# A decoder layer on one core: value products one step later, and qk, v and the rotary k in other steps

## The reference, cut to what matters

```python
x = _layernorm(x + _L0_attn_ref(x, w_project, w_out))        # causal, 16 heads of 16
x = _layernorm(x + _L0_xattn_ref(x, ctx_2048, Wq, bq, Wk, bk, Wv, bv, Wo, bo))
x = _layernorm(x + _L0_ffn_ref(x, w1, b1, ln_g, ln_b, w2, b2))
...
# cross attention: x and ctx are (32, 64, 256), read as 64 channels of length 256
q = _apply_rotary(q_emb, split_heads(_proj(x, Wq, bq)))      # 8 heads of 8 channels
k = _apply_rotary(k_emb, split_heads(_proj(c, Wk, bk)))
v = split_heads(_proj(c, Wv, bv))
p_attn = softmax(einsum('bhtc,bhsc->bhts', q, k) / sqrt(8))  # 256 x 256 per head
out = _proj(einsum('bhts,bhsc->bhtc', p_attn, v))
```

## Time and profile before

| what | value |
|---|---|
| profiled execution | 563.8 us, span 561.9 us |
| PE busy | 450.6 us (80%) |
| DVE busy | 442.4 us (79%) |
| ACT busy | 382.0 us (68%) |
| POOL busy | 289.6 us (52%) |
| mean granted TensorE clock | 0.848 |

### The profile page before, as it was taken

How to read it: one execution, slowest core, us unless ns; L and a number is a source line. 1 busy time by engine, 2 the same in 40 slices (tenths; PEclk the granted TensorE clock), 3 DMA queues, 4 the chain that set the end, 5 groups by cost and what they waited for, 6 DMA issues and landing times. The chain is left out here.

```text
span 561.9 us, 12026 instructions
## 1 busy us (share of the span) xinstructions
PE 450.6 (80%) x4162; PEld 243.0 (43%) x4162; DVE 442.4 (79%) x965; ACT 382.0 (68%) x698; POOL 289.6 (52%) x387
## 2 busy tenths in 40 slices
PE   6568799999999999999999999889877701555563
PEld 5354545555545555555555555433333200333342
DVE  2656687888988979889889798865848959999973
ACT  2222266767767667676676686687767787999972
POOL 5742565447555574475555744620032727667652
PEclk9677799999999999999999999975987875555555
DMA  6134318233242242332422323210000000000010
GB/s 217 48 97 149 97 46 248 66 92 91 57 111 67 64 110 60 90 91 60 108 69 64 106 61 82 71 56 1 3 1 1 1 0 1 10 28 19 30 37 29
DMA packets 51674, 37.07 MB, mean 66 GB/s; under 512 B 21408, under 2 KB 47648, under 8 KB 51488
## 3 DMA queue, kind: packets, MB, share of 16 engines
q1 hardware_dynamic: 51328, 36.10, 22.8%
q10 hardware_dynamic: 288, 0.23, 0.2%
HBM read 24.52 MB, written 10.49 MB: 62 GB/s over the span
## 5 line engine op out<-in xcount | busy, mean ns | idle before, releaser
L970 DVE TENSOR_REDUCE MX<-mx_b 128x2 f32<-128x512 f32 x256 | 167.8, 679 | 37.6 <-PE mx_b L581 36.4
L775 ACT ACTIVATE PB<-e_b 128x512 f32<-128x512 f32 x256 | 149.6, 592 | 64.7 <-PE e_b L609 63.8
L581 PE MATMUL mx_b<-KA,QA 48*128 48x256 bf16 x512 | 100.8, 282 | 10.3 <-DVE MX L970 10.1
L609 PE MATMUL e_b<-QA,KA 50*128 50x256 bf16 x512 | 100.9, 281 | 2.7 <-ACT PB L775 2.1
L626 PE MATMUL u_b<-PB,VA 128*32 128x256 f32 x1024 | 86.2, 404 | 3.4 <-ACT PB L775 2.9
L897 POOL TENSOR_TENSOR SP<-SP,srec 128x1024 f32<-128x1024 f32 x15 | 28.5, 1901 | 79.0 <-DVE srec L942 79.0
L581 PEld LDWEIGHTS mx_b<-KA,QA 48*128 48x128 bf16 x512 | 30.1, 95 | 88.5 <-issue 48.9
L1238 POOL TENSOR_TENSOR H<-H,row_tab 128x1024 f32<-128x1024 f32 x16 | 37.8, 2359 | 22.9 <-ACT H L1196 19.5
L1285 PE MATMUL r_b<-identh,Q 128*128 128x128 f16 x128 | 16.6, 311 | 39.5 <-ACT Q L1206 39.5
L1291 PE MATMUL z_b<-w2q,Q2T 128*128 128x256 bf16 x128 | 30.2, 417 | 19.3 <-ACT Q2T L1217 19.3
L314 POOL TENSOR_TENSOR rs<-mv,epsc 128x1 f32<-128x1 f32 x32 | 6.1, 189 | 72.5 <-DVE mv L301 50.2
(11 more groups left out here) (169 smaller groups left out, 1048.4 us busy)
## 6 DMA issues: line engine op xcount, KB each, us to landing
KA<-parts_k SPq DMA_DIRECT2D x64, 96.0 KB
QA<-parts_q SPq DMA_DIRECT2D x64, 96.0 KB
parts_q<-part_q SPq DMA_DIRECT2D x32, 128.0 KB, 2.0
parts_k<-part_k SPq DMA_DIRECT2D x16, 192.0 KB, 2.1
C<-in_ctx SPq DMA_DIRECT2D x16, 128.0 KB, 3.0
X<-in_x SPq DMA_DIRECT2D x16, 128.0 KB, 2.9
out_y<-O SPq DMA_DIRECT2D x16, 128.0 KB, 1.7
XT<-in_xT SPq DMA_DIRECT2D x15, 128.0 KB, 2.2
```

The source lines that it names most:

```text
L581: m = nc.tensor.matmul(mx_b[n % 2][:, D * k:D * k + D], QA[low:low + K_MAX, 2 * i.ring + b, h, P * u:P * u + P], KA[low:low + K_MAX, 2 * i ...
L609: m = nc.tensor.matmul(e_b[n % 2][:, D * k:D * k + D], KA[low:low + K_EXP, 2 * i.ring + b, h, P * sc:P * sc + P], QA[low:low + K_EXP, 2 * ...
L775: nc.scalar.activation(PB[:, n % 4].rearrange("p e t -> p (e t)"), e_b[n % 2][:, :], ACT.Exp, scale=XC ** -0.5).then_inc(e_sb.sem, 1)
L970: nc.vector.tensor_reduce(MX[:, b, e, 2 * q:2 * q + 2, u], mx_b[n % 2][:, :].rearrange("p (e s) -> p e s", e=2), AXL.X, ALU.max).then_inc( ...
```

## The change

On PE the quads 0 to 6 move from the even steps 2 to 14 to the odd steps 3 to 15, each behind the other blocks of its step, and quad 7 of the pair before moves from step 0 to step 1. `qk_proj` moves from step 1 to step 0, `rotary_proj("k")` from step 9 to step 8, `v_proj` from step 12, where it stood ahead of `transpose_p`, to step 14. On ACT the two `u_copy` move from steps 0 and 8 to steps 1 and 9. DVE's, POOL's and SP's lists in a body stay as they are. In the prologue a small table (`identb`) is made by two copies in place of one addition, and the counts of the semaphore s_tab are raised by one.

```diff
-                    if s == 0 and real(prev):
+                    if s == 0 and fresh(a):
+                        qk_proj(a, g_b[2])
+                    if s == 1 and real(prev):
                         pv_quad(prev, 7)
-                    if s == 1 and fresh(a):
-                        qk_proj(a, g_b[2])
...
-                    if s == 9 and fresh(a):
+                    if s == 8 and fresh(a):
                         rotary_proj("k", g_b[2], a)
...
-                    if s == 12 and real(i.plus(4)):
-                        v_proj(i.plus(4), g_b[0])
...
+                    if s == 14 and real(i.plus(4)):
+                        v_proj(i.plus(4), g_b[0])
                     if s == 15 and real(a):
                         out_proj(a)
-                    if s and s % 2 == 0 and real(i):
+                    if s >= 3 and s % 2 and real(i):
                         pv_quad(i, s // 2 - 1)
...
-                pe.wait_ge(s_tab, 2)
+                pe.wait_ge(s_tab, 3)
...
-                    if s == 0 and real(prev):
-                        u_copy(prev, 1)
...
+                    if s == 1 and real(prev):
+                        u_copy(prev, 1)
...
-                    if s == 8 and real(i):
+                    if s == 9 and real(i):
                         u_copy(i, 0)
...
-            nc.vector.tensor_tensor(identb[:].rearrange("p (b t) -> p b t", b=2),
-                                    ident[:, 0:HALF].unsqueeze(1).broadcast_to([P, 2, HALF]),
-                                    ident[:, HALF:P].unsqueeze(1).broadcast_to([P, 2, HALF]), ALU.add).then_inc(s_tab, 1)
+            for r in range(2):
+                own = slice(HALF * r, HALF * r + HALF)
+                nc.vector.tensor_copy(identb[own, :].rearrange("p (b t) -> p b t", b=2),
+                                      ident[own, own].unsqueeze(1).broadcast_to([HALF, 2, HALF])).then_inc(s_tab, 1)
...
-            pe.wait_ge(s_tab, 3)
+            pe.wait_ge(s_tab, 4)
```

## The result

The changed kernel took 594.38 us (median of six runs, 592.97 to 598.53) against 564.68 us before in the same runs. The ratio is 1.053, with a 95% interval of 1.047 to 1.059. The forecast was 595. The profiled execution of the changed kernel took 593.7 us with a span of 591.8.

The account below looks back on a forecast made before the run. The prediction took bodies 0 to 12 to be paced by DVE's softmax chain, for which PE waits, not by PE's busy time. It summed 563.8 + 27.7 + 2.1 + 1.5 = 595 us, range 578 to 612.

Parts of the forecast that it names:

- The walk through a body: Start times from a full body's first head through steps 0 to 15, ending at 25.03 us against 22.50.
- The +2.5 us a body: Bodies 1 to 11: 1.63 for quad 5 and `v_proj` behind step 13's wait, with 0.89 from step 13 starting later.
- the length of the body: Sign named in advance: bodies of the changed kernel repeat every 25.0 us.
- the wait of step 7: Sign: PE waits 1 us or more for DVE's maximum ahead of step 7's heads.
- the gap of DVE: Sign: DVE has a gap ahead of the maximum of step 9, where it had none.
- The wait for POOL: Sign at `transpose_p` on PE: it waits 1.3 us or more for POOL in each full body.
- stay at 1.00: Sign: PE's clock stays at 1.00 in the changed kernel.
- the moves ahead of `scores`: Steps 0 to 3: the same blocks in another order, costed at nothing; `scores` stays at 6.62.
- The prediction's own term for step 13: Heads of step 13 wait for DVE's maximum of step 11: 18.84 + 0.74 = 19.58, against 18.69 before.
- Body -1, the last three bodies ... I cost at nothing: No self-attention chain in the last three, same PE work: costed at nothing, bounded by 1.6 us either side.
- Body 0: First full body: +2.1 us, since it has no `norm2_stats` and the 0.46 falls away.
- The clock rival: PE's clock falls to 1.2 GHz, some 2 us a body in three to thirteen bodies, 601 to 621 us; chance 0.17.

Follow-up runs that it names:

- half division: The changed kernel with POOL's self-attention division done for only 8 of the 16 heads: 591.3 us, ratio 1.044 to the kernel before.
- new last bodies: The kernel before with the new order of quads and their copies in bodies 13 to 15 alone: 558.4 us, ratio 0.989.
- old last bodies: The changed kernel with the old order of quads and copies in bodies 13 to 15: 601.0 us, ratio 1.065 to the kernel before.
- even quads: The changed kernel with quads 0 to 6 and the first copy back in the even steps: 598.9 us, ratio 1.061 to the kernel before.
- `v_proj` in the gap: The changed kernel with `v_proj` back in step 12, ahead of `transpose_p`: 577.7 us, ratio 1.022 to the kernel before.

## Why the prediction was right, and where it was only right in sum

**The walk through a body** held step by step. Counted from the body's first head (222.00), foretold and measured: step 7 at 10.64 and 10.66, step 8 at 12.17 and 12.20, step 9 at 13.56 and 13.58, `self_sum` 14.59 and 14.62, the end of the division 18.07 and 18.10, `transpose_p` 18.15 and 18.15, the maximum of step 11 at 18.84 and 18.87, step 13 at 19.58 and 19.58, end 25.03 and 24.97. The +2.5 us a body measured 2.47. Of the signs named in advance, the length of the body, the wait of step 7 and the gap of DVE are there. Two are not as foretold. The wait for POOL is 1.04, not 1.3 or more, because PE comes to it at 17.11 and not at 16.6 to 16.9: step 9 took 1.53 instead of 1.43, and from step 10 to the first block of step 12 it took 1.94, above the 1.87 that I had as the most. And the clock did not stay at 1.00 in all bodies.

**The parts.** Taking `v_proj` back gives 1.16 us (1.06 was foretold), the rotary k 0.78 (1.06), the quads with their copies 0.34 (0.4, worked out for the experiment), the moves ahead of `scores` cost 0.03 (nothing). The single gains of the first two add to 1.94, and both at once give 24.96 - 23.23 = 1.73. They nearly add since each shortens a different stretch: the one ahead of `transpose_p`, the other behind step 13.

**"The wait for POOL" was named as idle time, not as the price**, and rightly. The half division shows that POOL's lateness alone is worth 0.07 us, since two other releasers stand just behind it. The prediction's own term for step 13 was the maximum of step 11, 19.58. Both stand on the same late tile.

**"Body -1, the last three bodies ... I cost at nothing" failed.** The last bodies gained some 6 us. I had looked for the self-attention chain there, which is absent, and held that equal work of PE takes equal time. But PE's work there runs at 1.2 GHz for long stretches, after waits behind ACT's two weight sums, and how long depends on the order. The rows were in the trace of before: the 1.32 us wait and the slow quads after it. I read them as the price of a low clock, not as something that the change might mend. The bound that I gave this part, 1.6 us, was far too small.

**Body 0** was foretold at +2.1 and took +5.5, with PE at the low clock twice. Without these two falls, at 1.49 each, it is the +2.5 of the other bodies, so the 0.46 that I took off for the absent `norm2_stats` did not show. The stretch ahead of `scores` of body 0 is 2.2 us longer, and part of that is scatter from one execution to the next. The kernel with new last bodies, whose code up to there is that of the kernel before, reaches `scores` at 73.17 instead of 72.14; the one with old last bodies, which is the changed kernel up to there, at 73.96 instead of 74.36. The two copies of the table took 2.05 us together, where I had reckoned with one more operation of 0.29. They stayed hidden all the same: its first use comes at 10.70 to 11.71 in the eight kernels with the copies and at 10.70 to 11.49 in the five with the addition.

**The clock rival** came true at its low end. It stood at 0.17 on three to thirteen bodies at 2 us, 6 to 26 us in all. The clock fell in three of the 13 full bodies, twice in body 0, at 1.49 us each: 6.0 us, which the forecast did not have. The page "TensorE: Matmul & The Clock Gate", section "HAM oscillation — how this bites in real kernels", of the Trainium skill describes a loop in which the clock falls in each trip, behind waits for DMA of 3 to 5 us. In this trace the waits are of about 1 us and for other engines; they stand in every body, and most bodies keep the full clock.

So the time agreed to within a microsecond by the median, and to 1.4 by the profiled execution that the sum was made for, because what I left out cancelled: 2.2 (start) + 3.4 (body 0) + 3.0 (two clock falls) against 0.8 (body 1 of the kernel before had lost that much on its own), 0.5 (eleven bodies at 2.47 and not 2.52) and 8.6 from body 12's softmax to the end, which came out 7.1 shorter where the forecast had it 1.5 longer. The sum had the right mechanism and the right main term. That the rest, more than 8 us on either side, came out at nearly nothing was luck.

## What to carry to other kernels

Where an engine in order waits for another at a fixed point, ask of each moved block on which side of that point it lands: from ahead of it to behind it costs the block's whole time, and the wait grows by as much. The length of a wait is not its price: ask what would hold the same instruction, and the next ones, if that releaser came in time. A late tile costs more on the engine that must take it before something urgent than on the one that made it; look at what stands behind it in that engine's list, and remember that a block also covers the evacuation that follows it. Walk the last trips of a loop by themselves: they have other waits, and an order that is bad for the middle can be right for the end.

## What the runs showed of the hardware

Each of these figures is from one profiled execution of a kernel. In bodies 1 to 12 PE's granted clock fell in the changed kernel (waits of 1.04 and 0.33 us on either side of the transposes; bodies 5 and 10), in the one with the old last bodies (the same waits, and the same two bodies), in the half division (0.92 and 0.49; 3 bodies) and in the even quads (0.71 and 1.04; 4 bodies). It did not in those with 0.62 and 0.39, with 0.55 and 0.49, or with `v_proj` in the gap. The undisturbed bodies of one kernel are alike to a hundredth of a microsecond, and yet some fall and others don't, so how the waits lie in a body doesn't settle it alone. A fall cost 1.43 to 1.50 us each time in these bodies, while in body 13 of the kernel before PE stayed at 1.2 GHz for 19.8 us although it was busy for 19.0 of them, and with the new order of the last bodies it was back at 2.4 GHz after some 4 us (376.6 to 380.2).
